# One semaphore per sum and per block step, one count in all passes, and places unpacked without an AND, in a graph network kernel on one core

## The reference

```
h = maximum(layernorm(x), 0);  x = x + segment_sum(sqrt(in_norm * out_norm) * h[src], dst)   # layer 0
h = ...;  x = x + two AGNN layers(h)    # p = softmax over the edges of a node of beta*cos(h[src], h[dst])
                                        # relu(segment_sum(h[src] * p, dst)), twice
h = ...;  x = x + segment_sum(h[src] @ W_a[type16], dst)                                      # layer 2
h = ...;  x = x + segment_sum(h[src] @ W_b[type32], dst) / degree + h @ W_self + bias          # layer 3
```

## Time and profile before

| what | value |
|---|---|
| median of 3 runs | 16,613.94 us (16,609.46 to 16,620.77) |
| the profiled execution | 16,705.54 us, its span 16,703.7 us |
| busy in the span | PE 7,120.6 us, PE weight loads 6,075.7, DVE 6,471.3, ACT 2,680.9, POOL 9,403.8 |
| passes 0 to 4, us from the span's start | 2,795 to 5,430; 5,430 to 8,470; 8,470 to 11,600; 11,625 to 14,250; 14,253 to 16,700 |

### The profile page before, as it was taken

The page is one execution under the profiler, slowest core; times in us unless marked ns, Lnnn a source line. Parts: engine busy times, 40 slices in busy tenths (PEclk is TensorE's granted clock), DMA queues, the critical chain, the costliest instruction groups (busy, mean ns, idle before and its releaser), DMA issues. The chain is left out here.

```text
span 16703.7 us, 167845 instructions
## 1 busy us (share of the span) xinstructions
PE 7120.6 (43%) x35085; PEld 6075.7 (36%) x35140; DVE 6471.3 (39%) x18639; ACT 2680.9 (16%) x7299; POOL 9403.8 (56%) x9933
## 2 busy tenths in 40 slices
PE   4311112222222566666656666665333334333333
PEld 1100001222222555555555555554323233223323
DVE  3322224333333455555545555554222223222222
ACT  0000000000000333333333333333000000000000
POOL 5476763655555555555545555554656656566666
PEclk5555555555555555555555555555555555555555
DMA  1000001111111111111121111112111112111111
GB/s 29 3 5 5 5 4 44 22 21 21 21 21 19 37 36 39 36 36 39 36 38 42 46 42 42 43 42 37 39 38 40 40 38 44 31 23 23 23 23 22
DMA packets 429667, 499.79 MB, mean 30 GB/s; under 512 B 235856, under 2 KB 245584, under 8 KB 417584
## 3 DMA queue, kind: packets, MB, share of 16 engines
q0 software_dynamic: 317504, 279.59, 10.7%
q1 hardware_dynamic: 97730, 214.09, 3.8%
q10 hardware_dynamic: 14316, 4.81, 0.1%
HBM read 397.49 MB, written 94.54 MB: 29 GB/s over the span
## 5 line engine op out<-in xcount | busy, mean ns | idle before, releaser
L680 POOL DMA_INDIRECT Z<-table,idx x4986 | 4703.3, 943 | 4326.8 <-issue 1700.3
L1575 PE MATMUL ps<-Z 128*128 128x65 f32 x9972 | 2313.9, 419 | 4972.2 <-DVE pay_d L1367 2504.1
L1575 PEld LDWEIGHTS ps<-Z 128*128 128x128 f32 x9972 | 2189.5, 329 | 5209.0 <-issue 5065.3
L1367 DVE SCALAR_TENSOR_TENSOR pay_d<-pay_d,ps 128x65 f32 x4986 | 1110.2, 223 | 4000.0 <-issue 2976.3
L680 POOL DMA_INDIRECT Z<-table_a,idx x1662 | 1567.8, 943 | 1090.1 <-issue 549.0
L656 POOL DMA_INDIRECT bins_dst<-slot_d x1612 | 1561.5, 969 | 959.4 <-issue 495.7
L680 POOL DMA_INDIRECT Z<-table_b,idx x1662 | 1567.9, 943 | 894.1 <-issue 514.6
L1562 PE MATMUL ps<-Z 128*128 128x65 f32 x6648 | 1532.9, 418 | 275.1 <-DVE pay_d L1214 213.1
L1562 PEld LDWEIGHTS ps<-Z 128*128 128x128 f32 x6648 | 1468.5, 331 | 361.1 <-DVE Z L1202 240.0
L1529 PE MATMUL ps<-pay_d,Z 128*128 x6648 | 1532.9, 421 | 33.2 <-ACT Z L738 31.1
L1529 PEld LDWEIGHTS ps<-pay_d,Z 128*128 128x128 f32 x6648 | 1485.5, 333 | 32.4 <-issue 32.1
(11 more groups left out here) (245 smaller groups left out, 7975.3 us busy)
## 6 DMA issues: line engine op xcount, KB each, us to landing
pay_d<-locals_ SPq DMA_DIRECT2D x92, 1152.0 KB
Z<-table,idx POOLq DMA_INDIRECT x4986
table_b<-pay_d SPq DMA_DIRECT2D x192, 256.0 KB
Z<-table_a,idx POOLq DMA_INDIRECT x1662
Z<-table_b,idx POOLq DMA_INDIRECT x1662
bins_dst<-slot_d POOLq DMA_INDIRECT x1612
table_a<-kept SPq DMA_DIRECT2D x94, 256.0 KB
slot_d<-pay_d SPq DMA_DIRECT2D x62, 91.0 KB
```

The lines of the kernel that those rows point to most:

```text
L680: nc.gpsimd.indirect_dma_start(rows[:, at.slot, j, 0:width], None, ps_.table, bass.IndirectOffsetOnAxis(ap=idx[:, at.slot, j:j + 1], axis= ...
L1367: v.scalar_tensor_tensor(out=of_block, in0=of_block, scalar=1.0, in1=p_pair[:, at.two, j * ROW:(j + 1) * ROW], op0=ALU.mult, op1=ALU.add). ...
L1575: last = mm(p_pair[:, at.two, j * ROW:(j + 1) * ROW], hot_d[:, at.three, j, :], given, start=True, stop=True)
```

## The change

Six semaphores `item_added` take the place of `part_added`, `added`, `sum_part` and `sum_added`: sum j signals `item_added[j]`, sum j > 0 waits for `item_added[j - 1]`, and `added` is the last of them. All count one for a group and go on over all passes. `own` is gone: each wait takes `e`, and the semaphores that only softmax passes use start NG higher. `hot_f_made` serves both kinds of one-hots. `blk_step` becomes 15 semaphores, one for a step k, and `step_of` counts the blocks that have passed step k. An even place is made by shift, product and difference.

```diff
-        blk_step, blk_root = sem("blk_step"), sem("blk_root")
+        blk_steps = [sem(f"blk_step{k}") for k in range(1, 16)]
+        blk_root = sem("blk_root")
...
-        msg_made, summed, added, part_added = sem("msg_made"), sem("summed"), sem("added"), sem("part_added")
+        msg_made, summed = sem("msg_made"), sem("summed")
+        item_added = [sem(f"item_added{j}") for j in range(ITEMS)]
+        added = item_added[ITEMS - 1]
...
         def place_at(at, j):
             two = at.known[j // 2]
-            one = (two & 4095, two >> 12)[j % 2]
+            one = (two - (two >> 12) * 4096, two >> 12)[j % 2]
...
+        def blk_step(k):
+            return blk_steps[k - 1]
+
         def step_of(p, rank, k):
-            return rank.n * OPS[p] + (sum(OPS[:p]) * NB + k)
+            return rank.n + (sum(OPS[q] >= k for q in range(p)) * NB + 1)
...
-                    act.wait_ge(risen, done(own + at.g))
+                    act.wait_ge(risen, done(e + at.g))
...
-            for s in (factor_kept, hot_f_made, hot_f_direct, multiplied, dotted, scored, group_max, max_made, risen,
-                      shift_made, msg_made, added, sum_added):
+            for s in [factor_kept, hot_f_made, msg_made] + item_added:
                 dve.sem_inc(s, CREDIT)
+            for s in (multiplied, dotted, scored, group_max, max_made, risen, shift_made):
+                dve.sem_inc(s, CREDIT + NG)
...
                     def one_sum(at):
                         if j == 0:
                             dve.wait_ge(summed, done(e + at.g))
-                            dve.wait_ge(keep_made, done(own + at.g))
-                            dve.wait_ge(added, done(own + at.g - 1))
+                            dve.wait_ge(keep_made, done(e + at.g))
+                            dve.wait_ge(added, done(e + at.g - 1))
                         else:
-                            dve.wait_ge(part_added, (own + at.g) * (ITEMS - 1) + j)
+                            dve.wait_ge(item_added[j - 1], done(e + at.g))
...
-                    ins.then_inc(blk_step, 1)
-                    dve.wait_ge(blk_step, step_of(p, rank, k))
+                    ins.then_inc(blk_step(k), 1)
+                    dve.wait_ge(blk_step(k), step_of(p, rank, k))
...
                         if j == 0:
                             dve.wait_ge(summed, done(e + at.g))
-                            dve.wait_ge(sum_added, done(own + at.g - 1))
+                            dve.wait_ge(added, done(e + at.g - 1))
                         else:
-                            dve.wait_ge(sum_part, (own + at.g) * (ITEMS - 1) + j)
+                            dve.wait_ge(item_added[j - 1], done(e + at.g))
```

More of the change, by code:

```diff
@@ L379, in gnn_program, with __init__ @@
         class Pass:
-            def __init__(self, kind, every, gather, own, column=0, table=None):
+            def __init__(self, kind, every, gather, column=0, table=None):
                 self.p = every
@@ L716, in work @@
             def work(ps_):
-                e, own = ps_.every, ps_.own
+                e = ps_.every
                 def rows_wanted(at):
@@ L741, in exponentials @@
                 def exponentials(at):
-                    act.wait_ge(shift_made, done(own + at.g))
+                    act.wait_ge(shift_made, done(e + at.g))
                     act.wait_ge(summed, done(e + at.g - 2))
@@ L1171, in new_maxima @@
                     o = at.slot * ITEMS
-                    dve.wait_ge(group_max, done(own + at.g))
+                    dve.wait_ge(group_max, done(e + at.g))
                     v.tensor_tensor_scan(run[:, o:o + ITEMS], items(fresh, at), gmax[:, at.two, :], run_at(at, -1),
@@ L1177, in rises @@
                     o = at.slot * ITEMS
-                    dve.wait_ge(max_made, done(own + at.g))
+                    dve.wait_ge(max_made, done(e + at.g))
                     if at.slot == 0:
@@ L1193, in messages @@
                     if ps_.softmax:
-                        dve.wait_ge(exp_made, done(own + at.g))
+                        dve.wait_ge(exp_made, done(e + at.g))
                         to, factor = msg[:, at.two, :, :], p_exp[:, at.two, :]
@@ L1230, in whole @@
                     rank.place = known.with_bounds(min_val=0, max_val=(pl.banks - 1) * 512 + (PER_BANK - 1) * ROW)
-                    if ps_.softmax:
-                        dve.wait_ge(added, done(own + rank.last))
-                    else:
-                        dve.wait_ge(sum_added, done(own + rank.last))
+                    dve.wait_ge(added, done(e + rank.last))
                     return acc[:, bass.ds(rank.place, D)], acc[:, bass.ds(rank.place + D, 1)]
@@ L1428, in _ @@
         def _(pe):
-            for s in (dst_rows, spread, edge_max, summed):
-                pe.sem_inc(s, CREDIT)
+            pe.sem_inc(summed, CREDIT)
+            for s in (dst_rows, spread, edge_max):
+                pe.sem_inc(s, CREDIT + NG)
             for s in (part_made, blk_turned):
@@ L1520, in work @@
             def work(ps_):
-                e, own = ps_.every, ps_.own
+                e = ps_.every
                 def rows_of_destinations(at):
-                    pe.wait_ge(hot_32_made, done(own + at.g))
-                    pe.wait_ge(multiplied, done(own + at.g - 2))
+                    pe.wait_ge(hot_32_made, done(e + at.g))
+                    pe.wait_ge(multiplied, done(e + at.g - 2))
                     for j in range(ITEMS):
@@ L1566, in sums_per_node @@
                 def sums_per_node(at):
-                    pe.wait_ge(sum_added, done(own + at.g - 2))
-                    pe.wait_ge(hot_f_direct, done(own + at.g))
+                    pe.wait_ge(added, done(e + at.g - 2))
+                    pe.wait_ge(hot_f_made, done(e + at.g))
                     if ps_.scaled:
```

99 lines of the change are left out of this document (50 added, 49 removed).

## The result

The changed kernel takes 16,383.5 us (median of four runs, 16,368 to 16,388), the kernel before 16,611.7 us (four runs, 16,549 to 16,621): ratio 0.9869, 95% interval 0.9844 to 0.9894, or 228 us less. The forecast was 744 us less. The profiled executions differ by 325 us (16,705.5 and 16,380.9 us), and their passes show where. Up to 97 us of that are no gain: the profiled execution before is 94 us longer than the median of that kernel, the one after 3 us shorter. Differences of passes against the kernel before carry this.

A forecast was written before the change was run, and what follows sets the result against it. VectorE, waiting for its own instruction stream, was taken to hold POOL above 7.49 us a group. Savings of 532 us (direct passes) and 210 us (softmax), 742 us, off 16,613.9 us gave 15,870 us; range 15,450 to 16,500 us.

The forecast's parts named there:

- What bounds the kernel: In the five edge passes POOL's floor is 7.49 us a group; VectorE is late, waiting for its own instruction stream.
- What the change removes: VectorE's instructions per group, with block share, fall from 40.7, 32.5, 28.8 to 30.5, 23, 20.5 in passes 0, 3, 4.
- The dearer unpacking: Between wait and sum at VectorE's even places, shift and subtraction replace the AND; counted as nothing, at most 436 us.
- Rival 4: Slower: unpacking by division, before VectorE's sums at even places, is dearer than the AND, 0 to 436 us; chance 0.06.
- the rule that fetches are hidden: A sequencer's instruction fetch hides behind issue, so VectorE's register instructions beside a sum are free everywhere; no chance given.
- The stock: VectorE's instructions, filled while POOL stops, drained while it gathers: 62 in a fast stretch, slow supply 1.37 a us.
- reading A: VectorE's stock drains during POOL's gathers; fewer instructions save 532 us in direct, 210 us in softmax passes: 15,870 us; chance 0.45.
- B: VectorE's fast stretch lasts a fixed 9 us; saves 179 us in direct, 134 us in softmax passes: 16,300 us; chance 0.28.
- The step that failed: Direct passes: n VectorE instructions a group set L groups a cycle; saves 0.63, 0.71 and 0.77 us a group, 532 us.
- The softmax passes: In passes 1 and 2 VectorE's slow stretch, once a round, shortens by 2.5 us; times 84 rounds, 210 us.
- The proof that wasn't: Runs without a profile are 0.55% lower, so VectorE's slow stretches were taken as no product of profiling.
- rival 2: VectorE's demand falls below the stock's need, slow stretches vanish: direct passes save 1,348 us, softmax 590 us; 14,680 us; chance 0.08.

The follow-up runs named there:

- the AND kept: Changed kernel with the AND back at the even places, semaphores as changed; ratio to the kernel before 0.9832, on a chip without the hold 0.9995.
- TensorE halved: Changed kernel with the sums' matmuls of passes 3 and 4 on 16-bit operands, one weight load and matmul an item; ratio to the kernel before 0.9832.
- 12.3 a group: Changed kernel with VectorE's sums of passes 3 and 4 added at fixed columns, so no places are read; ratio to the kernel before 0.9858.

## Why the prediction was wrong, step by step

**What bounds the kernel.** Right as far as it went: POOL's floor of 7.49 us would hold all passes but for a hold on the other engines while POOL gathers. Where there is no hold, the passes are at 7.6 to 7.8 us a group and the execution at 12,795 us. Wrong in who is held: "VectorE is the late one, and it waits for its own instruction stream". TensorE's signal is held as well. The 222 us of "remote" before the sums, in the waits of pass 4, stood below the rows that I took.

**What the change removes.** Right: the lines and counts above. The dearer unpacking was the one term on the path taken at nothing, with bounds of 0 and 0.105 us for each even place. It is 0.084 us more at an even place and 0.051 us less at an odd one, with the first sum's 0.10 us a group. Rival 4 has its mechanism, not its size: 0.10 x 831 = 83 us over the direct passes if nothing hid it, and pass 0 shows 54 us, against 23 us that pass 3 gains.

**Is it the fetch?** The prediction sets the rows of 0.70 us against the rule that fetches are hidden. The trace has two queues of instruction packets, and in 2,000 us in the middle of pass 4, after, they moved two packets between them (`--dma`, 14,100 to 16,100 us):

```profile
q0 software_dynamic: 44320, 45.47, 10.5%
q14 instruction: 2, 0.02, 0.0%
```

So the slow instructions there, 271 register instructions of more than 0.6 us in the pass, don't go with fetched packets; which engines' the two queues are, the trace doesn't tell. The Trainium skill ("Runtime: NRT & Kernel Launch", Instruction fetch mechanics) has the fetch hidden by the time an instruction takes to issue. On the two chips without the hold the trace agrees (longest 0.225 us before a sum); on the others, with up to 1.40 us, nothing in it shows a fetch as the cause.

**The stock.** From the start of a burst to the first slow instruction in pass 4 VectorE ran, in the median burst that has one, 53 instructions in 7.8 us before, 59 in 10.0 with the AND kept, 59 in 12.0 with TensorE halved, 69 in 18.5 after, where only 42 of the 68 bursts have one. Less 1.37 a us these are 42, 45, 43 and 44. So a stock that is drawn down at reading A's supply fits all four, and the fast stretch did grow past 12 us, against B.

**The step that failed** is the one after it: that a cycle holds as many groups as VectorE's stock allows, "after: n = 20.5, L = 5.4, 8.26 us", 0.63 us less a group. It made VectorE's count the only thing that ends a burst. With a third fewer instructions L was 4.0 instead of 5.4, and even with 12.3 a group the median burst was of four, ended at TensorE's held signal. The stop, taken as 4.2 us in any case, was 5.0 us. An instruction of VectorE was priced at 0.63 / 8.3 = 0.076 us a group in pass 4; there it is worth 0.010 to 0.013 us: 8.85 to 8.75 us for eight. B's 16,300 us lies closest to the 16,384 us, but its fixed stretch of 9 us isn't what happens, and that its 179 us for the direct passes are near the 171 us measured is luck: it had 0.26, 0.26 and 0.19 us a group for passes 4, 3 and 0, and 0.10, 0.46 and 0.05 us were measured. Pass 0, priced at 0.77 us a group, gave 15 us in all: by the one profile with the AND kept the semaphores gave 69, and the AND's removal took 54 back.

**The softmax passes.** The slow stretch did go, where I had it shortened: of 299 and 329 register instructions of more than 0.6 us in passes 1 and 2 none is left. But a round of pass 1 is 64.8 us in place of 65.1: VectorE now waits for TensorE's sums until 2.6 us after each burst's end. A round of pass 2 fell from 67.7 to 64.6 us. What ends the burst there stays open.

**The proof that wasn't.** "That the runs without a profile are so close says that the slow stretches are no product of profiling": every run here comes with a recorded span and clock, so the nearness proves nothing, and the runs leave open whether recording has a part in the hold. That the floor could be reached (rival 2, priced for a smaller demand) was true of another chip, not of this change.

**Open.** What is filled while POOL gathers and emptied when it stops, and why the time of pass 4 hardly moves with the counts. Why two of the chips don't show it is open too: each was used at one time only, the two last of all, so chip and time can't be told apart. Shown is that the gathers bring it, that a stop of 1.2 us a group keeps it away in passes 3 and 4, and that it takes both VectorE's stream and TensorE's signals.

## What to carry to other kernels

Where an engine waits for "issue", look for the wait that stands next in the same table, however small: a removed one is taken over by it. Before pricing a stall by one engine's count, take that engine's work nearly away in one run; here that would have shown 8.7 us a group in pass 4, not 7.49. And run the kernel before on more than one chip: a gain of 1.3% on one chip was nothing on two others.

## What the runs showed of the hardware

- The same kernel, at the same granted clock of 0.50, takes 16,612 to 16,667 us on some chips and 12,802 and 12,814 us on two others.
- In the hold a matmul's recorded end and the signal it raises lay 21.7 us apart in the burst shown, and VectorE's longest wait for it in pass 4 was 29.7 us, while DMAs keep their time: a gather's last packet ends 2.05 us after its issue in the first and in the thirtieth us of a burst.
- TensorE's own semaphore instructions last 0.05 us by the median. In passes 3 and 4 of the changed kernel 24 of 417 took more than 0.6 us, up to 2.0; with a stop of POOL, or on a chip without the hold, none took more than 0.051 us.
- A signal from VectorE to TensorE isn't late in the same burst: the last sum ends at 15,020.33, and TensorE's wait for it is over at 15,020.37.
- After a stop POOL's first gather starts 0.77 us after its wait is over (15,036.69 and 15,037.46).
- A fused register instruction of VectorE took 0.046 to 0.053 us without a shift, 0.092 to 0.104 us with a shift in front, and 0.209 us for shift, multiply, subtract, multiply and add.
